# Norm sums moved ahead of the gating, and a new issue order for a two-head softmax attention, in a fused four-layer kernel

## The reference, cut to what matters

```python
h = h + _L0_ffn_ref(_layernorm(h), ...)     # 16 experts
h = h + _L1_attn_ref(_layernorm(h), ...)    # one head per sequence
h = h + _L1_ffn_ref(_layernorm(h), ...)     # 4 experts
h = h + _L2_attn_ref(_layernorm(h), ...)    # 16 linear heads
h = h + _L2_ffn_ref(_layernorm(h), ...)     # 8 experts
h = h + _L3_attn_ref(_layernorm(h), ...)    # 8 heads
h = h + _L3_ffn_ref(h, ...)

def _layernorm(x):
    m = mean(x); v = var(x)
    return (x - m) / sqrt(v + eps)

def _L1_attn_ref(x, Wq, Wk, Wv):            # per sequence, 512 x 64
    att = softmax(q @ k.T, axis=-1) * 64 ** -0.5
    return att @ v
```

## Time and profile before

| | |
|---|---|
| median of 3 runs | 909.41 us (908.62 to 911.94) |
| the profiled execution | 908.61 us, span 906.8 us |
| mean granted TensorE clock in it | 0.957 |
| TensorE matmuls busy | 794.8 us, 88% |
| VectorE busy | 641.0 us, 71% |
| ScalarE busy | 367.0 us, 40% |
| GpSimd busy | 241.0 us, 27% |
| L1 attention | about 286 to 334 us of the span |
| end of the L1 experts and L2 attention | about 442 to 487 us |
| end of the L2 experts, start of the L3 attention | about 515 to 532 us |

### The profile page before, as it was taken

The page is one execution under the profiler, slowest core; times in us unless marked ns, Lnnn a source line. Parts: engine busy times, 40 slices in busy tenths (PEclk is TensorE's granted clock), DMA queues, the critical chain, the costliest instruction groups (busy, mean ns, idle before and its releaser), DMA issues. The chain is left out here.

```text
span 906.8 us, 21880 instructions
## 1 busy us (share of the span) xinstructions
PE 794.8 (88%) x9110; PEld 417.8 (46%) x9110; DVE 641.0 (71%) x1720; ACT 367.0 (40%) x633; POOL 241.0 (27%) x308
## 2 busy tenths in 40 slices
PE   0897879979999887997978989999999988888997
PEld 0566757755544335774445423333333333344443
DVE  3988648887897448998776885556565557666665
ACT  0213354444664243323444614555554432353443
POOL 1900003222645212441362041113133325110000
PEclk9898989998999999999899999999999999987999
DMA  9500030000000001000000000000000000000000
GB/s 280 170 1 2 1 98 3 3 3 2 1 2 2 1 2 50 1 2 1 1 1 2 1 2 1 1 3 2 1 2 1 2 1 3 3 2 1 7 7 13
DMA packets 11501, 15.40 MB, mean 17 GB/s; under 512 B 8390, under 2 KB 9446, under 8 KB 10406
## 3 DMA queue, kind: packets, MB, share of 16 engines
q1 hardware_dynamic: 9984, 12.91, 4.6%
q10 hardware_dynamic: 1418, 1.09, 0.5%
HBM read 13.47 MB, written 0.52 MB: 15 GB/s over the span
## 5 line engine op out<-in xcount | busy, mean ns | idle before, releaser
L1001 DVE TENSOR_REDUCE mx<-PS 128x2 f32<-128x1024 f32 (+3 forms) x96 | 103.1, 1088 | 65.8 <-PE PS L776 54.6
L947 ACT ACTIVATE arena<-PS 128x1024 f32<-128x1024 f32 (+3 forms) x96 | 85.8, 917 | 119.4 <-PE PS L820 107.7
L810 PE MATMUL PS<-arena 32*64 32x512 f32 (+3 forms) x768 | 86.3, 563 | 8.8 <-DVE mx L1001 2.9
L836 PE MATMUL PS<-arena 128*64 128x512 f32 (+3 forms) x384 | 91.1, 558 | 0.4 <-DVE arena L1060 0.4
L776 PE MATMUL PS<-arena 32*64 32x512 f32 (+3 forms) x768 | 85.6, 563 | 0.9 <-DVE mx L1001 0.4
L1543 ACT ACTIVATE arena<-PS,f_b_sb 128x512 f32<-128x512 f32 x96 | 61.1, 684 | 39.6 <-PE PS L1474 36.9
L1571 DVE TENSOR_TENSOR arena<-arena,PS 128x512 f32<-128x512 f32 x96 | 61.6, 683 | 15.6 <-PE PS L1485 15.5
L1474 PE MATMUL PS<-XT,late 64*64 64x512 f32 x384 | 63.0, 619 | 2.9 <-issue 1.5
L1505 PE MATMUL PS<-arena,late 64*64 64x512 f32 x384 | 57.9, 595 | 0.0
L1105 POOL TENSOR_TENSOR H<-H,arena 128x256 f32<-128x256 f32 x32 | 23.5, 733 | 114.3 <-DVE arena L1035 111.8
L1755 DVE TENSOR_TENSOR arena<-arena,PS 106x512 f32<-106x512 f32 (+1 forms) x48 | 30.8, 684 | 20.9 <-PE PS L1655 13.7
(11 more groups left out here) (482 smaller groups left out, 1718.4 us busy)
## 6 DMA issues: line engine op xcount, KB each, us to landing
arena<-in_rel SPq DMA_DIRECT2D x4, 1024.0 KB, 11.9
late<-in_edges SPq DMA_DIRECT2D x2, 1024.0 KB, 11.8
arena<-in_adj SPq DMA_DIRECT2D x1, 1024.0 KB, 6.8
late<-in_w_f_w SPq DMA_DIRECT2D x2, 512.0 KB, 3.9
Cc<-in_consts SPq DMA_DIRECT2D x1, 916.0 KB
arena<-in_ids ACTq DMA_DIRECT2D x1, 800.0 KB
late<-in_w_f_w SPq DMA_DIRECT2D x2, 340.0 KB, 3.7
late<-in_w_f_w SPq DMA_DIRECT2D x4, 128.0 KB, 2.9
```

The lines of the kernel that those rows point to most:

```text
L810: ins = nc.tensor.matmul(PS[half(m), a + j, queries(g, c)], KT[h, g % 3, of_chunk(c, m)], QT[h, g % 3, queries(g, c)], start=not less_firs ...
L836: ins = nc.tensor.matmul(PS[half(j), 6 + p, queries(g, c)], XO[:, batch(g) * TB + c, :], PT[:, s % 2, p, j, queries(g, c)], start=c == 0, ...
L947: nc.scalar.activation(PT[:, s % 2, p, :, queries(g, c)], PS[:, a:a + 2, queries(g, c)], ACT.Exp, scale=of(g).scale).then_inc(exp_done.sem, 1)
L1001: v.reduce_max(mx[:, g % 2, c, 2 * p:2 * p + 2], PS[:, a:a + 2, keys(g, c)], axis=AX.X).then_inc(max_done.sem, 1)
```

## The change

Four edits, with no operation added or taken away but three fillers.

1. In `experts` with T = 4, `after.sums` of quarters 0 to 2 moves right behind the quarter's two additions, ahead of the gating of that step and of the half sum.
2. In `l2_attn`, TensorE turns quarter 2 after `kv(1)`, `queries(0)`, `queries(1)` and no more before `kv(1)`; ScalarE copies it after the first square; VectorE's `root` of quarter 3 moves one place up, from behind step (2,0) to behind (1,0).
3. In `softmax_attention` the order on TensorE becomes: rows 0 to 3, turn of quarter 2, 3 fillers (6 before), maxima(0), cols 0, cols 1, mix 0, turn of quarter 3, proj(1), cols 2, mix 1, rows 4, rows 5, cols 3, mix 2, rows 6, rows 7, mix 3, maxima(1), cols 4, cols 5, mix 4, and on as before. Before, the turn of quarter 3 and proj(1) stood ahead of cols 0 and behind maxima(0), one `rows` stood between each two steps, and mix 3 followed cols 4. ScalarE's copies follow, and its copy of the first group's context comes before the maxima's copy.
4. GpSimd's `values_out(0)` and `values_out(1)` move into the norm of quarter 3, behind `apply` of its first norm and behind `centre` of its second.

```diff
+        first, later = new_in(1)
+        units = [("N", q, 0) for q in new_in(0)] + [("P", 0, 0)] + [("A", s, 0) for s in range(TB)]
+        units += [("N", first, 0), ("T", 0, 0), ("B", 0, 0), ("B", 1, 0), ("N", later, 0), ("P", 1, 0)]
+        units += [("B", 2, 0), ("A", TB, 0), ("A", TB + 1, 0), ("B", 3, 0), ("A", TB + 2, 0), ("A", TB + 3, 0), ("T", 1, 0)]
+        units += [("B", TB, 0), ("B", TB + 1, 0), ("O", 0, 0), ("B", TB + 2, 0), ("B", TB + 3, 0), ("O", 1, 0)]
...
                 entered.turn(eng, first, slot(("N", first, 0)))
-                unread(6, a=7)
-                entered.turn(eng, later, slot(("N", later, 0)))
+                unread(3, a=7)
                 maxima(0)
-                proj(1)
                 eng.wait_ge(out_added.sem, before["out_added"])
                 eng.wait_ge(xo_ready.sem, at(xo_ready, 1))
...
+                cols(0)
+                cols(1)
+                mix(0, 0)
+                entered.turn(eng, later, slot(("N", later, 0)))
+                proj(1)
+                cols(2)
+                mix(1, 0)
+                rows(TB)
+                rows(TB + 1)
+                cols(3)
+                mix(2, 0)
+                rows(TB + 2)
+                rows(TB + 3)
+                mix(3, 0)
+                maxima(1)
+                for s in range(TB, U):
+                    cols(s)
+                    if s > TB:
                         mix(s - 1, 0)
...
+                    if s == TB + 1:
+                        outs(0, 0)
+                mix(U - 1, 0)
...
+                    if s == 1:
+                        entered.turned_out(eng, later, bank(("N", later, 0)))
+                        qk(1)
+                    if s == 3:
+                        contexts(0)
+                        maxima(1)
...
-                if len(entered.norms) > 1:
-                    entered.centre(eng, B - 1, 1)
-                    entered.apply(eng, B - 1, 1)
-                for b in range(B):
+                values_out(0)
+                entered.centre(eng, B - 1, 1)
+                values_out(1)
+                entered.apply(eng, B - 1, 1)
+                for b in range(2, B):
                     values_out(b)
...
+        short = T == 2 * LAG
...
+                        if after is not None and short and b < B - 1:
+                            eng.wait_ge(out_added.sem, a0 + b + 1)
+                            after.sums(eng, b, 0)
...
-                            if e == 0:
+                            if e == 0 and not short:
...
                 kv(0)
-                entered.turn(eng, 2, turn_bank(2))
                 kv(1)
                 queries(0)
                 queries(1)
+                entered.turn(eng, 2, turn_bank(2))
                 kv(2)
...
-                for q in range(B - 1):
+                for q in range(2):
                     entered.turned_out(eng, q, turn_bank(q))
...
+                        if q == 0:
+                            entered.turned_out(eng, 2, turn_bank(2))
...
-                    if (k, q) == (2, 0):
+                    if (k, q) == (1, 0):
                         entered.root(eng, B - 1, 0)
```

More of the change, by code:

```diff
@@ L379, in _ @@
                     rows(s)
-                first, later = new_in(1)
                 entered.turn(eng, first, slot(("N", first, 0)))
-                unread(6, a=7)
-                entered.turn(eng, later, slot(("N", later, 0)))
+                unread(3, a=7)
                 maxima(0)
-                proj(1)
                 eng.wait_ge(out_added.sem, before["out_added"])
                 eng.wait_ge(xo_ready.sem, at(xo_ready, 1))
[L388 to L395, removed]
-                        mix(s - 1, 0)
[L397 to L414, removed]
+                cols(0)
[16 more added lines that the diff above has]
+                    if s > TB:
+                        mix(s - 1, 0)
+                    if s == TB + 1:
+                        outs(0, 0)
+                mix(U - 1, 0)
                 unread(4, a=bank(("B", U - 1, 0)))
@@ L441, in turned_out @@
                         entered.turned_out(eng, q, bank(("N", q, 0)))
[L443 to L447, removed]
+                turned_out(0)
+                qk(0)
+                entered.turned_out(eng, first, bank(("N", first, 0)))
                 maxima(0)
-                for g in range(early, 2):
-                    qk(g)
                 for s, (g, c) in enumerate(steps):
-                    for p in range(NPAIR):
-                        a = bank(("B", s, p))
-                        eng.wait_ge(cols_done.sem, at(cols_done, s * NPAIR + p))
-                        nc.scalar.activation(PT[:, s % 2, p, :, queries(c)], PS[:, a:a + 2, queries(c)], ACT.Exp, scale=scale).then_inc(exp_done.sem, 1)
-                    if s == 0 and weights is not None:
-                        eng.wait_ge(products_done.sem, p0 + 1)
-                        nc.scalar.copy(weights["out"], PS[0:D, bank(("W", 0, 0)), 0:len(weights["pairs"]) * D]).then_inc(products_copied.sem, 1)
-                    if c == 0 and g >= 1:
-                        contexts(g - 1)
-                    if c == 0 and g + 2 < G:
-                        turned_out(g + 2)
-                    if c == 2 and g + 2 < G:
-                        qk(g + 2)
-                    if c == 3 and g + 1 < G:
-                        maxima(g + 1)
+                    eng.wait_ge(cols_done.sem, at(cols_done, s))
+                    a = bank(("B", s, 0))
+                    nc.scalar.activation(PT[:, s % 2, 0, :, queries(c)], PS[:, a:a + 2, queries(c)], ACT.Exp, scale=scale).then_inc(exp_done.sem, 1)
+                    if s == 1:
[4 more added lines that the diff above has]
+                        maxima(1)
                 contexts(G - 1)
```

25 lines of the change are left out of this document (removed).

## The result

The changed kernel takes 913.65 us (median of 20 runs, 910.77 to 917.11) against 909.46 us before (20 runs, 903.5 to 918.14). The ratio is 1.0044, 95% interval 1.0026 to 1.0063: 4.0 us slower, 2.4 to 5.7. Forecast were 910.2 us, a range of 906.5 to 914.0, and no change by more than 0.5%. The time is in the range, 0.35 us from its slow end, and the change of 0.44% is under 0.5%, though its interval reaches 0.63%; it is five times the 0.8 us of the sum.

What follows compares the result with a forecast made beforehand. TensorE is busy 88% of the span, so only seams where it or its feeder idles can give time. 908.6 + 0.15 - 1.9 + 2.6 = 909.5 us, on the median 910.2; range 906.5 to 914.0.

Steps and rivals of the forecast that it cites:

- The sums: Experts with T = 4: earlier sums let the additions of quarter 3 in the L1 experts start 1.4 us earlier.
- The price of `sums` itself: Experts, VectorE: about 0.82 us between a quarter's second addition and what comes next.
- The L2 attention: Together with the earlier sums, -1.9 us up to the end of this stage, between 0 and -2.2.
- The L3 projection: Start of the L3 attention: `proj` starts 0.15 us later, between 0 and +0.8, as the turn of quarter 0 becomes the later input.
- The L1 attention: The new order on TensorE brings the last mix 2.6 us later, bounds -1.5 and 3.9.
- the hole of about 2 us ahead of the second maxima: L1 attention: TensorE idles about 2 us before maxima(1), with cols 4 starting at 322.85 against 318.97.
- the part that comes back: L1 attention: some of the 3.9 us lost up to cols 4 returns by the last mix, leaving +2.6.
- half the clock, as in the rows before: L1 attention behind the first maxima: half clock assumed, cols 0 from 303.7 to 305.8, cols 1 to 307.0.
- the signs that were named: L1 attention, among others: rows 7 ending 3.6 us later, last mix 2 to 3 us later against the turn of quarter 0.
- Rival A: L1 attention: the clock stays low longer (1.6 us) and falls in the second hole (1.8 us); 913.6 us, chance 0.16.
- Rival B: L1 attention: the new order pays, its term between -1.5 and 0; 906.1 to 907.6, say 907 us, chance 0.18.
- Rival C: The sums do nothing, GpSimd or the table load hold the L2 attention where it was; 912.1 us, chance 0.10.

Runs made afterwards that it cites:

- e3: The kernel before with only the earlier sums in the experts, both attentions as before; 908.95 us, ratio 1.0007.
- e2: The kernel before with the earlier sums and the L2 attention's edits, L1 attention untouched; 911.14 us, ratio 1.0000.
- e4: The changed kernel with 24 unread filler matmuls in place of 3 before the first maxima of the L1 attention; 912.53 us, ratio 1.0024.
- e12: The changed kernel again without any edit, in another execution, for its trace; L1 attention 44.42 us, no whole time given.

## Why the prediction was right or wrong

**The sums: right.** Additions of quarter 3 were to start 13.35 us after the first ones, and do after 13.38. `turn(2)` on TensorE was put 0.49 later and came 0.77 later (9.15 after the first additions, 8.38 before); `root` of quarter 1 without a wait, 9.02 against 8.73 forecast. The price of `sums` itself, 0.82 us, is right for neither quarter. For quarter 0 of the L2 experts, second addition to gating went from 0.54 to 1.03 us, 0.5 more; for quarter 1 of the L1 experts it went from 0.34 (449.45 - 449.11) to 1.39 (455.51 - 454.12), 1.05 more. There the second operation of the sums took 0.56 us in place of 0.17: it starts at 455.04, 0.08 behind a GpSimd operation of 0.61, and ends with it (455.60 and 455.57); e3's trace has the same pair. The prediction didn't have this, and its 0.39 us more than cover the 0.28 by which `turn(2)` is later than forecast.

**The L2 attention: right.** After the first additions, forecast and measured: epsilon step (2,0) 18.7 and 18.72; bias step (0,2) 20.8 and 20.70; (0,3) 24.55 and 24.29; GpSimd's long addition 24.9 and 24.78, 2.0 us earlier than before, and the epsilon step still ends with it. The gain is 2.22 us (2.48 in e2) where 1.9 was said, 2.0 of it up to GpSimd's addition and the rest in the piece behind it, which varies with the clock. The Trainium skill ("SBUF — State Buffer", Who interferes with whom) gives the port pair that VectorE shares with GpSimd as the reason why the step ends with the addition, and lets the engine that issued first go first; the 2.31 us row agrees, and GpSimd started 0.11 to 0.56 us ahead in all 14 traces, so the other order was never seen.

**The L3 projection: the size is inside the bounds.** First additions of the L2 experts to the projection: 12.62 before (528.62 - 516.00), 12.68 after (533.27 - 520.59), +0.06 for +0.15. As said, the later input is now the turn of quarter 0. TensorE's timeline of the kernel after, where the experts' last turn waits for nothing (0.79 us in the earlier trace rows):

```profile
531.49 1.09 PE L2261 MATMUL PS<-Cc,X 128*64 128x128 f32 x16
532.56 0.66 PE L1476 MATMUL PS<-Cc,arena 128*128 128x128 f32 x4
533.27 1.13 PE L728 MATMUL PS<-XT,late 64*128 64x512 f32 x4
```

**The L1 attention: the mechanism right, one term too small.** The 0.7 us ahead of the projection is 0.73, the hole of about 2 us ahead of the second maxima is 1.91, the part that comes back 1.25 (forecast 1.3). But cols 4 start 36.54 us after the last turn; forecast were 34.65, before it was 30.77. The 1.9 us lie ahead of the turn of quarter 3, at half clock. The first maxima's transposes and their copy run into it, so cols 0 start 1.62 us after the split (302.74 - 301.12) and not 1.21: 0.4. Cols 0 to the turn of quarter 3 was put at 4.3 us, with cols 1 half warm and mix 0 warm; it took 5.79: 1.5. In e4, at a clock of 1.00, the same piece takes 3.44, so the prediction had allowed 0.9 us for the low clock there, and it cost 2.35. Behind that the parts miss by +0.2, -0.7 and +0.55 and cancel. The step that was mis-sized is "half the clock, as in the rows before": the low stretch was taken over from a trace in which the wait ahead of it was 3.48 us, while the new order makes it 5.02. e4 prices the whole of it at 2.56 us; 0.2 of that lies ahead of cols 0, which makes 1.7 of the 1.9 us the clock's. The other 0.2 isn't: in e4 too cols 0 start 1.41 us after the split and not 1.21. So two of the signs that were named missed: rows 7 end 5.5 us later and not 3.6, and the last mix comes 4.5 us later against the turn of quarter 0 and not 2 to 3.

That the layout was right in sum is partly luck: its parts miss by up to 0.7 us and cancel.

**Rival A** described it. Its first half, 1.6 us for a low stretch until 310, came as 1.9 until 308. Its second half, a drop in the second hole, isn't in the kernel after and is in e4: 1.4 us where 1.8 was put. The argument against it, that a shorter hole didn't drop the clock before, carried nothing, since the same hole does and doesn't. At 0.16 its first half had too little, with a wait worked out at 4.8 us, longer than the one that had already dropped the clock. That its time, 913.6 us, is almost the measured median of 913.65 is luck: it has 1.8 us for a second drop that the trace doesn't show, and none of the 1.7 us outside of the two stretches.

**Rival B** fell: the order doesn't pay, and costs 3.2 us even with the low stretches filled (42.09 against 38.89). Rows 4, which feed the second maxima, wait behind cols 0 to mix 1. **Rival C** fell by the stretches of e2 and e3, though not by their times, which show no gain.

**The total.** Forecast for the profiled execution 909.5, measured 914.05, 4.6 us more: 1.9 in the L1 attention, -0.3 in the L2 stretch, and 3.0 outside of both, where the sum had 0.15 and 14 traces vary by 11 us. Against the medians, +4.0 where +0.8 was said: 1.6 from the two stretches; the rest, with an interval of 1.6 us either side, isn't settled. The forecast was for no change above 0.5%, and that held; but the median stayed in the range by 0.35 us, with one term 1.9 us too small and 1.7 us outside of both stretches that the sum didn't have. That it didn't fall outside is luck.

## What to carry to other kernels

Price a reorder by the work that feeds the next gate, here the row maxima of the second group, not by what is ready first: filling the first wait's end with cols and mix put rows 4 6.9 us later after the stage's start (26.59 for 19.67) and opened a hole of 1.9 us. Where a reorder lengthens a wait of TensorE that already drops the clock, take the matmuls behind it at half speed until a run shows otherwise, and try unread matmuls through the wait before a new order: 14 of them were worth 1.24 us of that stage, though not of the whole time that could be measured (-0.2 us, -2.5 to 2.2). Measure an edit of 2 us by the distance between two events of its stage, in the trace, and the whole only to see that nothing else turned. Read the clock over that distance too: the L2 stretch varied by 1.2 us with its code untouched (42.50 to 43.69), and its pieces were long where the clock was low.

## What the runs showed that was not expected

A hole of 1.91 us with 0.38 us of transposes and 0.68 us of nothing behind them left TensorE's clock at 1.00 in the kernel after and brought it to 0.55 in e4. The same kernel in two traces had low stretches in different waits of the same stage (0.56 in 342 to 344 after, 1.00 in 344 to 346 in e12), and runs of the kernel before spread from 903.5 to 918.1 us. A VectorE operation that needs the one before it was cheaper inside the loop than at its end: from the start of the second addition to the start of the sum that needs it 0.46 us, where the same pair took 0.67 us with a wait of 0.24 at the end of a step (458.87 in the earlier trace rows, behind an addition that starts at 458.20).
